# A later wait ahead of the first four groups' scatters in an embedding, attention and mixture-of-experts kernel

## The reference, cut to what matters

```python
h = _L0_tok_ref(x, 2, coeff_weight, base_embed_weight, lang_bias)      # softmax(coeff[x]) @ bases
h = h + _L0_attn_ref(_layernorm(h), Wv, bv, Wo, bo)                    # q = k = v, 16 heads of 16
h = h + _L0_ffn_ref(_layernorm(h), moe_router, moe_w13, moe_w2)        # top 2 of 8 experts
...
topk_logits, topk_idx = jax.lax.top_k(router_logits, TOP_K)
sort_idx = jnp.argsort(expert_ids, axis=0)
token_ids_sort = token_ids[sort_idx]
w13_out = jax.lax.ragged_dot(x_sort, moe_w13, group_sizes)
gate, up = jnp.split(w13_out, [MOE_DIM], axis=-1)
hidden = jax.nn.silu(gate) * up
out_dispatch = jax.lax.ragged_dot(hidden, moe_w2, group_sizes)
out_flat = zeros.at[token_ids_sort].add(out_dispatch * w_sort[:, None])
```

## Time and profile before

| what | us |
|---|---|
| median of three runs | 885.01 |
| the three runs | 883.3, 885.01, 887.09 |
| profiled execution, its own time | 876.52 |
| span of the profiled execution | 874.7 |
| end of attention's exponentials in it | about 543 |

### The profile page before, as it was taken

How to read it: one execution, slowest core, us unless ns; L and a number is a source line. 1 busy time by engine, 2 the same in 40 slices (tenths; PEclk the granted TensorE clock), 3 DMA queues, 4 the chain that set the end, 5 groups by cost and what they waited for, 6 DMA issues and landing times.

```text
span 874.7 us, 16526 instructions
## 1 busy us (share of the span) xinstructions
PE 764.2 (87%) x5200; PEld 299.7 (34%) x5250; DVE 502.4 (57%) x1575; ACT 544.7 (62%) x515; POOL 354.7 (41%) x305
## 2 busy tenths in 40 slices
PE   3699994999899999989999998189999999999992
PEld 2233220222222222222222222035555555555551
DVE  7624563566668448676656468755554555545540
ACT  0468993999999999989999997312222222222220
POOL 6760030311420330241233116356666666666752
PEclk9999996999999989999999999579999999999997
DMA  2030105012011101201110123349899999999973
GB/s 40 2 94 2 37 12 38 13 37 74 13 37 50 49 8 43 74 14 37 49 50 14 37 73 86 99 81 169 158 160 162 158 163 166 160 163 155 162 121 39
DMA packets 141362, 67.72 MB, mean 77 GB/s; under 512 B 114822, under 2 KB 136984, under 8 KB 141294
## 3 DMA queue, kind: packets, MB, share of 16 engines
q1 hardware_dynamic: 125262, 49.33, 27.5%
q0 software_dynamic: 16032, 17.55, 13.9%
HBM read 22.52 MB, written 17.57 MB: 46 GB/s over the span
## 4 chain that ended last, share of the span: by engine, by line
PE 69%; DVE 16%; ACT 5%; issue 5%; another core or an unknown queue 2%; DMA 1%; POOL 0%; SPq 0%; POOLq 0%; ACTq 0%; DVEq 0%
PE PS L360 20%; PE PS L1471 19%; PE PS L1480 10%; PE PS L348 9%; ACT shared L759 4%; PE PS L403 2%; DVE room L789 2%; PE PS L380 2%; DVE room L795 2%; PE PS L404 2%; DVE room L787 2%; PE PS L446 1%; DVE room L791 1%; PE PS L387 1%
## 5 line engine op out<-in xcount | busy, mean ns | idle before, releaser
L759 ACT ACTIVATE shared<-PS 128x1536 f32<-128x1536 f32 x342 | 465.0, 1513 | 50.3 <-PE PS L348 38.0
L360 PE MATMUL PS<-shared,va 128*32 128x512 f32 x2048 | 281.1, 622 | 5.1 <-DVE room L1244 4.6
L638 POOL DMA_INDIRECT slots<-pair_no,room x60 | 59.5, 991 | 366.5 <-DVE room L916 352.7
L1471 PE MATMUL PS<-w_p,room 128*128 x783 | 185.2, 380 | 1.7
L348 PE MATMUL PS<-room,ak 32*128 32x512 bf16 x1024 | 137.9, 397 | 18.1 <-ACT shared L759 9.7
L1521 ACT ACTIVATE shared<-PS 128x512 f32<-128x512 f32 x68 | 40.6, 597 | 163.2 <-PE PS L1471 163.2
L1437 POOL DMA_INDIRECT out<-room,idx_tok x68 | 110.7, 1628 | 66.0 <-ACT room L1526 37.9
L1552 DVE SCALAR_TENSOR_TENSOR shared<-shared,room,PS 128x512 f32<-128x512 f32 x68 | 50.9, 748 | 123.9 <-ACT shared L1521 123.9
L1471 PEld LDWEIGHTS PS<-w_p,room 128*128 128x128 f16 x816 | 79.8, 98 | 83.2 <-issue 0.8
L348 PEld LDWEIGHTS PS<-room,ak 32*128 32x128 bf16 x1024 | 33.4, 91 | 216.7 <-ACT shared L759 167.6
L1480 PE MATMUL PS<-shared,room 128*128 x816 | 101.4, 274 | 7.0 <-issue 5.1
(11 more groups left out here) (279 smaller groups left out, 599.6 us busy)
## 6 DMA issues: line engine op xcount, KB each, us to landing
room<-w SPq DMA_DIRECT2D x24, 512.0 KB, 4.7
xrows<-room SPq DMA_DIRECT2D x16, 258.0 KB, 3.4
out<-room SPq DMA_DIRECT2D x16, 256.0 KB
room<-room SPq DMA_TRANSPOSE x135, 3.9
room<-xrows,idx_tok POOLq DMA_INDIRECT x68, 4.1
out<-room,idx_tok POOLq DMA_INDIRECT x68
slots<-pair_no,room POOLq DMA_INDIRECT x60, 6.9
xT<-xT SPq DMA_DIRECT2D x3, 256.0 KB, 4.5
```

What stands on the lines that cost most here:

```text
L360: last = pe.matmul(PS[32 * slot:32 * slot + 32, ACC, :], g.va[:, KT * (grp // HG) + kt, c, :], prob[:, (4 * quad + slot) % (RING * WIDE), ...
L638: pool.indirect_dma_start(g.slots, bass.IndirectOffsetOnAxis(pos_i[:, grp % 2, 2 * k + kk:2 * k + kk + 1].bitcast(U32), 0), g.pair_no[:, t ...
L759: act.activation(prob[:, at:at + n, :].rearrange("p n q -> p (n q)"), PS[:, buf:buf + n, :].rearrange("p c q -> p (c q)"), ACT.Exp).then_i ...
L1471: last = pe.matmul(PS[:, up_bank(k) + half, :], xsT[:, k, 2 * a + c, :], g.w13_p[:, w, c, ds(e, 1), FF * half:FF * half + FF].rearrange("p ...
```

## The change

The threshold of one wait. `note(grp)` waited until the places of group `grp` were there. Now, for the groups 0 to 3, it waits until the places of group `grp + 1` are there as well; from group 4 on it is as it was. The number of instructions stays the same on every engine.

```diff
         def note(grp):
-            pool.wait_ge(pos_ready, grp + 1)
+            pool.wait_ge(pos_ready, grp + (2 if grp < HG else 1))
             for k in range(2):
                 for kk in range(2):
                     pool.indirect_dma_start(g.slots, bass.IndirectOffsetOnAxis(
```

## The result

The changed kernel takes 875.62 us (four runs, 873.8 to 877.16) against 884.15 us of the kernel before, in runs taken beside it (four, 882.11 to 887.09). The ratio is 0.990, with a 95% interval of 0.9865 to 0.9936: faster by 1.0%, and outside the range of 878 to 890. The profiled execution took 873.8 us, its span 872.0.

A forecast was written before the change was run, and what follows sets the result against it. The prediction took ACT's exponentials in attention as the bound. Pass 5's -2.78, pass 6's +2.57 and 0 for passes 2 to 4 made -0.2 us, so 885.01 became 884.8 us ("same"), with a range of 878 to 890.

The forecast's parts named there:

- What bounds the kernel: Attention, up to about 540 us: ACT's exponentials (465.0 us) set the pace, so each idle microsecond of ACT there counts.
- What the edit does to each queue: POOL's scatters and what follows them move by one release; waits of DVE, SP and PE on them cost nothing.
- The sum: All passes of attention: -2.78 + 2.57 + 0 = -0.2 us, with ends -2.8 and +2.3.
- Pass 5: DVE's group-loop turn 5: loses its two-piece release, so L795 is no longer slowed; -2.78 us.
- pass 6: DVE's group-loop turn 6: takes on the release whose second subtraction slows L795; +2.57 us.
- Rival 3: Third weight piece in pass 6 meets DVE, or later phases shift: +2.1 to +2.5 us, 887.2 us; chance 0.12.
- The 8.5 us: Whole kernel: unexplained excess of the timed runs' median, 885.01, over the profiled 876.52; carried over into the forecast.
- passes 2 to 4: 0: Turns 2 to 4: a piece less or another piece, where the trace shows no slowed instruction; 0 us.
- rival 1: Pass 2, 137 to 147 us: the stall hangs on group 0's scatters and goes with them; -13.9, 871.1 us; chance 0.11.
- the swap: Passes 5 and 6: the two-piece release and its hit on L795 move one pass later; -2.78 and +2.57 us.
- Rival 2: Pass 6: the stall hangs on how much the DMA queues hold and comes anew; 898.7 us; chance 0.09.

The follow-up runs named there:

- r5: The kernel before, unchanged, run once more for its trace; ratio 0.9997.
- r1: The changed kernel, run once more on the same chip; ratio 0.990 to the kernel before.
- r2: Kernel before with the scatters of groups 0 to 3 at their old release, but the values and weight pieces behind them one release later; ratio 1.0027.
- r4: Kernel before with only group 0's scatters waiting for one place more, the piece behind them moving along; ratio 0.9933.
- r13: Kernel before with group 0's four scatters left out, so that group's pairs are missing from the table; ratio 0.9917.
- r12: Kernel before with only group 7's scatters one release later, so that GpSimd's queue rests a second time; ratio 1.0048.
- r8: Kernel before with the scatters of groups 0 to 12, not only 0 to 3, waiting for one place more; ratio 0.9956.
- r3: Kernel before with the scatters of groups 0 to 3 one release later, values and weight pieces at their old release; ratio 0.9951.
- r11: Kernel before plus six blank scatters ahead of group 0's, four early and two later, to keep GpSimd's queue at work; ratio 0.9999.
- r7: Kernel before with the load of weight piece 3 moved behind the two stores that follow it on SP; ratio 1.0039.
- r14: Kernel before with group 0's scatters writing the blank value to the same cells at the same time; 885.99 us, one run.
- r6: Kernel before plus four early scatters of blank values into the table's first 512 cells, which group 0's scatters wait for; ratio 0.9959.
- r9: Kernel before plus four early scatters of blank values spread over the whole table, which group 0's scatters wait for; ratio 1.0003.
- r10: Kernel before with group 0's scatters held until the middle of pass 2, at 139.30 us; ratio 0.9952.
- r15: Kernel before with only the first of group 0's four scatters, the rest left out; 868.24 us, one run.
- r16: Kernel before with only the first two of group 0's four scatters; 879.81 us, one run.
- r17: Kernel before with only the last two of group 0's four scatters; 871.72 us, one run.
- r18: Kernel before with group 0's scatters split, two at the old release and two at the next, ahead of group 1's four; ratio 0.9873.

## Why the prediction was wrong

**What bounds the kernel**: right. ACT's idle time in attention fell, and the kernel became faster by about as much.

**What the edit does to each queue**: right. No scatter before 163, three pieces behind the release near 256, no wait of DVE for `noted`, no wait of SP for a buffer.

**The sum**: its mechanism was right for passes 5 and 6, and two sizes were off. Pass 5 was forecast to give back 2.78 and gave 1.7; pass 6 was forecast to take 2.57 and took 3.2. Of pass 5's three gaps in r5 (2.26, 0.76, 0.45 us) only the first shrank; r1 shows 0.51, 0.77 and 0.44, where the prediction had let all three sink to 0.69 together. Pass 6 of r1 shows 2.72 and 0.91 us where 2.11 and 0.95 had been taken. L795 took 2.50 us in pass 6 and 0.75 in pass 5:

```profile
235.98 0.75 DVE L795 SCALAR_TENSOR_TENSOR room<-room,part_c 128x512 bf16<-128x512 bf16 x1
...
264.98 2.50 DVE L795 SCALAR_TENSOR_TENSOR room<-room,part_c 128x512 bf16<-128x512 bf16 x1
```

The rule quoted from the Trainium skill ("SBUF — State Buffer", section "SBUF: two separate sides") agrees with these rows as with the earlier trace rows. The forecast of the sum was -0.2, measured +1.5. By itself that would still have been "same". Rival 3's price of 2.1 to 2.5 did not come: the gap of 1.04 us at 284.82, behind the third piece, stands in the kernel before as well, where there is no third piece:

```profile
282.24 8.19 ACT L759 ACTIVATE shared<-PS 128x1536 f32<-128x1536 f32 x6 [1.04 <-PE PS L348]
```

The 8.5 us that the forecast carried over from the profiled execution to the median were no part of its error. They are about the size of the hold-up in the start (131.16 - 123.38 = 7.8 us), which the profiled execution didn't have; that the unprofiled ones had it is likely and not shown.

**The step that failed** is the term "passes 2 to 4: 0" of the sum, and with it the weighing of rival 1. Measured (r5 to r1), pass 2 gave -12.5 us and pass 3 +2.0. The prediction saw the stall, priced it, and named the scatters as the one thing just ahead of it that the edit takes away; it then gave this 0.11, because 14 more groups have the same scatters and no stall. That argument asks why the scatters should do it only once, which is a fair question and still has no answer; but it doesn't bear on whether the edit moves the only cause in sight. r2 (scatters early, stall there), r4 (only they late, none) and r13 (only they missing, none) show that it hangs on them.

**Rival 1's size**: 13.9 us was taken as the difference between two passes with the same duties, and all of it as gone. Measured were 12.5 in pass 2, of which 2.0 came back in pass 3, and with the swap's 1.5 the net is about 9. "Goes with them" was wrong in its literal sense: the slow stretch moves with them, and the stall of the engines mostly doesn't.

**Rival 2** (slower, the stall anew in pass 6): wrong in its price, not quite in its mechanism. Eight scatters from 255 to 271, with a store and a load beside them, do bring a crawl, as the window 272 to 276 of the changed kernel shows (the queue, then the issues: KB, median us to landing):

```profile
q1 hardware_dynamic: 272, 0.31, 102.8%
...
room<-w SPq DMA_DIRECT2D x1, 512.0 KB, 10.6
xrows<-room SPq DMA_DIRECT2D x1, 258.0 KB, 10.2
```

Over all 24 loads and 16 stores of the kernel before the medians on the page are 4.7 and 3.4 us. The crawl ends near 284, 28 us behind the release at 255.44, and r1 has it too (122 packets and 126.8% from 260 to 264). r12's eight scatters from 388 to 401 brought none. No engine stood for it: pass 6 took 33.6 us here, and as much in r8, which has no such stretch there.

**Range and chances**: the range ended at 878, and rival 1 was left outside of it together with rival 2. The unexplained stall had been named the largest thing in the trace; a range that should hold 8 in 10 may leave out such a case only if the evidence against it is a measurement, and here it was an argument by analogy.

## What stays open

Why pass 2 pays 11 us of standing still and pass 3 only between 1.4 and 6.4 us in length (r8 30.0, r1 30.6, the changed kernel 32.0, r3 32.1, r4 35.0, against 28.6; r4's with the clock at 0.50 from 180 to 185) for the same stretch isn't shown. The engines' own instructions also come by DMA (queues 8 and 14 on the page, 35 and 33 packets in the kernel before), and "remote" is a releaser outside of the profile; an engine that runs out of instructions within the slow stretch would stand until its end, which fits that ACT and DVE begin again together at 147.28 and 147.23 (PE follows at 149.19, released by DVE). This was argued, not measured: r11 shows ACT standing up to 156.43 with no transfer of SP under way, so it is not SP's queue that they wait for.

The traces say a little more. Queue 8 brings instructions in packets of 16 KB. In six profiles with the stall (before, r2, r5, r7, r11, r14) such a packet starts within 1.6 us of the moment when ACT first stops, and it takes 3 to 5 us, where the median is about 1.1. The windows 136 to 140 of r5 and 144 to 148 of r11 (5.7% of 16 engines in 4 us is 3.6 us, 7.9% is 5.1):

```profile
q8 instruction: 1, 0.02, 5.7%
...
q8 instruction: 1, 0.02, 7.9%
```

In the changed kernel's pass 3 no instruction packet starts from 161 to 189 us, so none meets the crawl. That favours the theory. Against it: r6, r9 and r10 have the gap and no packet of queue 8 on record in it, r12's took only 1.8 us, r11's had landed 6 us before ACT went on, and packets of 3.4 and 3.1 us at 200 and 233 in r5 stop nobody.

Why it takes group 0's scatters, three or four of them, and group 1's four alone don't do it, is open too. Excluded are the data (r14, one run), first use of the table (r6, r9), a long rest (r11 and r12; and r13's first scatters came after as long a rest as the changed kernel's, at 163.43 and 163.17, without a crawl), the load (r7), and the pieces (r2). Not tried were other destination cells for group 0 at the same time, and three of the four. The Trainium skill, page "DMA: Bandwidth & Descriptors", section "Specifications", states that transfers under 512 B make the DMA engine read, modify and write. These scatters write 4 bytes each; but so do those of all groups, and if this rule alone were behind it, r13's first scatters at 163 would have slowed the transfers as well, which they didn't.

## What to carry to other kernels

If a trace holds a stall that it can't explain, and the edit moves the one thing just ahead of it, the stall's whole size belongs into the range, whatever speaks against the cause; the question how it works can stay open. A cause that sits a fixed time (here 23 to 27 us) ahead of its effect is found by moving the suspect and watching whether the effect keeps its distance. And a burst of small indirect writes is worth moving or splitting as an experiment: here either took the stall away (0.990 and 0.9873, not to be told apart), and neither would have been found from the cost of the scatters themselves.

## What the runs showed of the hardware

- Four scatters of 128 elements of 4 bytes, issued within 5 us, can leave a stretch in which SP's transfers move 30 to 44 packets in 4 us instead of some 400. It ends 23 to 27 us behind the first scatter, whatever the time of the scatters (ACT went on after 19 in r6, and in r18 the end belongs to the second lot), and by then their own packets have long landed, except in r10. With one or two of them it doesn't occur (r15, r16, r17), nor behind group 1's four alone (r13).
- The same stretch stops ACT for 11 us in one pass and for 2 to 3 us in the next (2.45 in the changed kernel).
- After 5 us with the same busy time of PE (3.28 us, r1 and r4) the clock was at 1.00 in one execution and at 0.50 in the other; in pass 2 this is worth 3.9 us. The same delay of 1.75 us on DVE made a pass 5.4 us longer in r12, with the clock at 0.50 for 10 us, than in the kernel before.
